# Perceiver block on one core: who spreads the softmax reciprocals over the columns, how Pool splits the second context, and where the second block of keys and values stands

## The reference

```python
q = split_heads(layernorm(x) @ Wq + bq)            # x: (2, 128, 512)
k = split_heads(ctx @ Wk + bk)                      # ctx: (2, 2048, 512)
v = split_heads(ctx @ Wv + bv)
attn = softmax(einsum('bhqd,bhkd->bhqk', q, k) / sqrt(32), axis=-1)
x = x + (einsum('bhqk,bhkd->bhqd', attn, v) as (2, 128, 512)) @ Wo + bo
x = x + self_attention(layernorm(x));  x = x + expert_ffn(layernorm(x))
```

## Time and profile before

| what | value |
|---|---|
| median of 3 runs | 535.88 us (535.83 to 538.25) |
| the profiled execution's own time | 539.55 us |
| its span, first to last instruction | 537.8 us |
| busy: PE, DVE, ACT, Pool | 514.9, 277.7, 248.9, 41.5 us |
| mean granted TensorE clock | 0.983 of full |

### The profile page before, as it was taken

One profiled execution on the slowest core, in us unless ns is written; L12 is line 12 of the kernel. 1 busy time (PEld: TensorE's weight loads), 2 busy tenths in 40 slices (PEclk: granted clock), 3 DMA queues, 4 the chain that ended last, 5 costly groups with the idle time before them and its releaser, 6 DMA issues.

```text
span 537.8 us, 9156 instructions
## 1 busy us (share of the span) xinstructions
PE 514.9 (96%) x3702; PEld 376.3 (70%) x3702; DVE 277.7 (52%) x570; ACT 248.9 (46%) x381; POOL 41.5 (8%) x56
## 2 busy tenths in 40 slices
PE   8989999999996999999999999898999999999995
PEld 5777777777774777888877778656665446877651
DVE  3676533645456552435385774530385537976232
ACT  4230128484945541237467567484164208655120
POOL 0130000000596000000000000000000010000000
PEclk9999999999997999999999999999999998999898
DMA  8800000000620022220400000781996964873000
GB/s 259 348 0 1 1 1 1 2 1 1 230 85 1 2 79 79 79 79 1 137 3 2 1 1 1 292 335 48 394 397 241 385 238 168 328 291 153 1 20 21
DMA packets 11746, 63.30 MB, mean 118 GB/s; under 512 B 1588, under 2 KB 2612, under 8 KB 4788
## 3 DMA queue, kind: packets, MB, share of 16 engines
q1 hardware_dynamic: 11704, 62.71, 30.9%
HBM read 62.18 MB, written 0.52 MB: 117 GB/s over the span
## 4 chain that ended last, share of the span: by engine, by line
PE 86%; ACT 7%; issue 2%; DVE 2%; DMA 1%; SPq 1%; POOLq 0%; DVEq 0%; ACTq 0%
PE ps L1004 36%; PE ps L1070 10%; PE ps L1259 10%; PE ps L1084 5%; PE ps L1058 5%; PE ps L1306 5%; ACT Pm L393 3%; PE ps L1286 3%; PE ps L1287 3%; PE ps L1288 3%; PE ps L998 1%; ACT PT L401 1%; DMA wv_raw<-in_xWv 1%; DVE rexp L666 1%; PE ps L1269 1%
## 5 line engine op out<-in xcount | busy, mean ns | idle before, releaser
L401 ACT COPY PT<-ps 128x512 f32<-128x512 f32 x128 | 68.8, 590 | 37.4 <-PE ps L1070 37.4
L655 DVE TENSOR_SCALAR_CACHE_REDUCE Pm<-ps,small 128x512 f32<-128x512 f32 x96 | 66.4, 748 | 29.4 <-PE ps L1058 29.2
L1070 PE MATMUL ps<-ident,Pm 128*128 128x128 f32 x512 | 69.7, 278 | 3.1 <-ACT Pm L393 2.2
L1070 PEld LDWEIGHTS ps<-ident,Pm 128*128 128x128 f32 x512 | 56.5, 141 | 18.4 <-issue 12.5
L393 ACT ACTIVATE Pm<-Pm,small 128x2048 f32<-128x2048 f32 x32 | 64.3, 2009 | 10.2 <-DVE Pm L655 10.1
L1259 PE MATMUL ps<-w1raw,z 128*128 128x512 f32 x128 | 57.3, 595 | 0.7 <-DVE Pm L655 0.7
L635 DVE SCALAR_TENSOR_TENSOR KrL<-ps,small,KrH 128x512 fp32r<-128x512 f32 x32 | 23.9, 747 | 56.8 <-ACT KrH L379 56.8
L1004 PE MATMUL ps<-ctxH,wkH 128*128 128x512 f32 x124 | 52.5, 423 | 0.0
L1004 PE MATMUL ps<-wvH,ctxH 128*128 128x512 f32 x124 | 49.8, 401 | 0.0
L1004 PE MATMUL ps<-ctxH,wkL 128*128 128x512 f32 x124 | 49.4, 399 | 0.0
L1004 PE MATMUL ps<-ctxL,wkH 128*128 128x512 f32 x124 | 49.4, 398 | 0.0
(11 more groups left out here) (169 smaller groups left out, 763.6 us busy)
## 6 DMA issues: line engine op xcount, KB each, us to landing
w1raw<-in_W SPq DMA_DIRECT2D x16, 1024.0 KB, 7.0
w2raw<-in_W SPq DMA_DIRECT2D x16, 1024.0 KB, 5.0
raw<-in_ctxT SPq DMA_DIRECT2D x7, 1024.0 KB, 4.9
woF<-in_ffn_Wo SPq DMA_DIRECT2D x4, 1024.0 KB, 12.3
wo<-in_wo SPq DMA_DIRECT2D x2, 1024.0 KB, 6.6
ctx_first<-in_ctxT SPq DMA_DIRECT2D x4, 256.0 KB, 5.0
wv_raw<-in_xWv SPq DMA_DIRECT2D x2, 512.0 KB, 6.9
wq<-in_xWq SPq DMA_DIRECT2D x1, 1024.0 KB, 12.0
```

The lines of the kernel that those rows point to most:

```text
L401: act.copy(PT[:, c % 2, i, :, :].rearrange("p k t -> p (k t)"), ps[:, T_BANKS[i % 2], :]).then_inc(pt_done, 1)
L655: dve.tensor_scalar(Pm[:, i, c * CH:(c + 1) * CH], ps[:, i, :], -1.0, mx[:, p % 2, i, c - 1:c] if c else NOT_YET, ALU.mult, ALU.min, accum ...
L1070: last = pe.transpose(ps[:, T_BANKS[i % 2], j * P:(j + 1) * P], Pm[:, i, c * CH + j * P:c * CH + (j + 1) * P], ident[:])
```

## The change

Four edits, and the wait counts that go with them:

1. `rexp`, the reciprocals spread over 32 columns a head, is written by a new ACT function `reciprocals(p)`, not by DVE. DVE's `reciprocals(p)` keeps only the four reciprocals. A new semaphore `recip_done` goes from DVE to ACT, and `rexp_done` now counts one a pass.
2. The place: DVE makes `reciprocals(p - 1)` behind `negative_scores(p, 2)` in every pass; before, it made those of pass `p - 2` at the loop's start, but for passes 4 and 8. ACT spreads them in chunk 3, between its second and third copy of transposed probabilities.
3. Pool splits each chunk of the second context with one cast and one subtraction of 128x2048, in place of four and four of 128x512.
4. The opening: PE makes `keys(0, 1)` ahead of the query projections, `values(0, 1, 0)` ahead of `scores(0, 0)`, and the other three blocks of values behind it. DVE and ACT take their part of `keys(0, 1)` ahead of their work on the queries.

```diff
@@ Pool
-                for k in range(KT):
-                    pool.tensor_copy(ctxH[c][:, k, :], raw[c][:, k, :]).then_inc(ctx_hi1, 1)
-                for k in range(KT):
-                    pool.wait_ge(ctx_hi1, KT * c + k + 1)
-                    pool.tensor_tensor(ctxL[c][:, k, :], raw[c][:, k, :], ctxH[c][:, k, :].bitcast(F32), ALU.subtract)\
-                        .then_inc(ctx_split1, 1)
+                pool.tensor_copy(ctxH[c][:], raw[c][:]).then_inc(ctx_hi1, 1)
+                pool.wait_ge(ctx_hi1, c + 1)
+                pool.tensor_tensor(ctxL[c][:], raw[c][:], ctxH[c][:].bitcast(F32), ALU.subtract).then_inc(ctx_split1, 1)
@@ ACT
+            keys(0, 1)
             act.wait_ge(bq_scaled, 1)
...
+            def reciprocals(p):
+
+                act.wait_ge(recip_done, p + 1)
+                if p:
+                    act.wait_ge(r_mm, p)
+                act.copy(rexp[:], recip.rearrange("p (h o) -> p h o", o=1).to_broadcast([P, HPG, DH])).then_inc(rexp_done, 1)
...
                         probs_T(p - 1, c, i)
+                        if c == 3 and i == 1:
+                            reciprocals(p - 1)
@@ DVE
             def reciprocals(p):
                 dve.wait_ge(exp_done, HPG * (p + 1))
-                dve.reciprocal(recip, den[:, p, :]).then_inc(rexp_done, 1)
-                dve.wait_ge(rexp_done, 2 * p + 1)
                 if p:
-                    dve.wait_ge(r_mm, p)
-                dve.tensor_copy(rexp[:], recip.rearrange("p (h o) -> p h o", o=1).to_broadcast([P, HPG, DH]))\
-                   .then_inc(rexp_done, 1)
+                    dve.wait_ge(rexp_done, p)
+                dve.reciprocal(recip, den[:, p, :]).then_inc(recip_done, 1)
...
-                if late:
-                    reciprocals(p - 2)
...
-                    if c == 2 and p in (G, NP):
+                    if c == 2:
                         reciprocals(p - 1)
@@ PE
-                pe.wait_ge(rexp_done, 2 * (p + 1))
+                pe.wait_ge(rexp_done, p + 1)
...
+            keys(0, 1)
             pe.wait_ge(xT_done, B)
             pe.wait_ge(wq_in, 16)
             for m in range(G):
                 product(ps[:, (m + 2) % 4, 0:TOK], [(wq[:, k, m * P:(m + 1) * P], xnT[:, k, :]) for k in range(KT)])\
                     .then_inc(q_mm, 1)
+            values(0, 1, 0)
             pe.wait_ge(q_split, G)
             scores(0, 0)
-            for c in range(1, C):
+            for j in range(1, JT):
+                values(0, 1, j)
+            scores(0, 1)
+            for c in range(2, C):
                 keys(0, c)
```

More of the change, by code:

```diff
@@ L214, in perceiver_block @@
         pt_done = sem("pt_done")
+        recip_done = sem("recip_done")
         pv_mm, rexp_done, r_mm, r_copied, o_done = (
@@ L426, in _ @@
             for c in range(1, C):
-                keys(0, c)
+                if c > 1:
+                    keys(0, c)
                 for j in (0, 2):
@@ L1010, in keys @@
                 if b:
-                    pe.wait_ge(ctx_split1, KT * (c + 1))
+                    pe.wait_ge(ctx_split1, c + 1)
                 else:
```

## The result

| | before | after |
|---|---|---|
| median | 537.07 us (535.83 to 539.99, 4 runs) | 529.95 us (528.53 to 530.43, 4 runs) |
| profiled execution, its span | 539.55, 537.8 us | 528.53, 526.8 us |
| mean granted clock in it | 0.983 | 0.998 |

The ratio is 0.9845, with a 95% interval of 0.9811 to 0.9879: 6.5 to 10.2 us saved. The two medians lie 7.1 us apart, inside that interval; one of the four executions of the changed kernel is the profiled one.

What follows compares the result with a forecast made beforehand. PE was taken to set the time, busy 514.9 of 537.8 us. Terms -7.3, +0.4 and -0.8 made -7.7 us, 539.55 to 531.9; less 3.67 from profile to median, 528.2, rounded to 528.4, range 526.6 to 531.4.

Steps and rivals of the forecast that it cites:

- The copy leaves DVE: Pass 4's start: without the held `rexp` copy, 5.21 us of PE gap and 2.15 of slow matmuls go; minus 7.3 us.
- ACT's copy 0.26 us, hidden but for 0.4 at pass 4's end: ACT's spread: idle time hides it before other passes' exponentials; pass 4's last weighted values wait, plus 0.4 us.
- rival B: ACT slips in every pass because its spread takes 1.2 us: 3.1 us lost, 531.5 us; chance 3%.
- The reciprocal is not held: Pass 3: DVE's reciprocals, moved into Pool's stretch, stay at 172 to 179 ns and cost nothing.
- rival D: Pass 3: Pool holds DVE's reciprocal in place of the copy, delaying the exponentials: 537.2 to 539.2 us; chance 2%.
- Edit 3 is worth zero: Pool's whole pieces end its run some 2 us sooner, but off PE's path: zero.
- The opening: PE gaps of 0.73 and 1.39 us go, one of 1.3 comes before the fourth values block: minus 0.8 us.
- rival C: Opening: DVE's copy of values comes in time and PE keeps the whole 2.1 us: 526.9 us; chance 8%.
- Minus 7.7 in all, 528.4 us: Whole kernel: -7.3 + 0.4 - 0.8 us, taken off the profile, then shifted to the median and rounded.
- Rival A: Pass 4's stall is smaller without the profiler: 531.9 us, or 530.3 with only the slow matmuls missing; chance 15%.

Runs made afterwards that it cites:

- e1: Kernel before, with only the reciprocals made a chunk sooner and spread by ACT; Pool in slices and opening as before: ratio 0.9887.
- e5: Changed kernel with Pool's split of the second context back in slices: ratio 0.9863.
- e3: Kernel before plus one wait: Pool starts the second context's chunk 3 only after DVE's copy to `rexp` of pass 2: ratio 0.9865.
- e2: Kernel before with reciprocals and the copy to `rexp` moved behind `negative_scores(p, 2)`, the copy still on DVE: ratio 1.0046.
- e4: Kernel before with only the new order of the opening: ratio 0.9984.
- e8: Changed kernel with the spread to `rexp` back on DVE, in the new place: ratio 0.9815.
- e10: Kernel before with DVE's reciprocals and copy moved behind `negative_scores(p, 2)`, each Pool cast slice followed by its own subtraction: 531.71 us, one execution.
- e11: Changed kernel with the spread back on DVE, and DVE's copy of `values(0, 1, 1)` put ahead of `split(2)`: ratio 0.9784.
- e12: Kernel before with DVE's reciprocals and copy moved behind `negative_scores(p, 2)`, Pool's casts whole, subtractions in four slices: 532.43 us, one execution.
- e9: Kernel before with DVE's reciprocals and copy moved behind `negative_scores(p, 2)`, Pool's casts and subtractions in halves of 1024 columns: 534.73 us, one execution.
- e7: Kernel before with only Pool's split in whole pieces: ratio 0.9876.

## Why the prediction was right, and where it was not

- *The copy leaves DVE: minus 7.3 us.* Right in mechanism and sum: 7.34 in the change, e1 and e5 (e3 shows the cause). The split is less right than it looks. From the gap's end to pass 4's scores the slow clock cost 10.15 - 7.67 = 2.5 us and not 2.15, since the 2.15 counts `keys(4, 1)` alone and the clock was at half to 175.22. Against that, a pass 4 that comes on time waits about 0.4 us for ACT's exponentials at the last transposes ahead of its scores, which the late pass hid. Both were left out, and that they cancel, so that 5.21 + 2.15 met 7.31, is luck.
- *ACT's copy 0.26 us, hidden but for 0.4 at pass 4's end.* It took 0.30, and PE waited 0.29 there; the other passes keep their 27.6 us, so rival B fell.
- *The reciprocal is not held* (rival D). Right: 173 to 179 ns, and 0.17 us ahead of the held copy in e2.
- *Edit 3 is worth zero.* Right beside edits 1 and 2 (e5), but the reason beside it was too broad. "The copy is held until Pool has finished its whole run of slices" was read from one copy. It holds for the order of the kernel before (also in e2 and e4); with whole pieces the wait ends with one instruction (e8), which is what the Trainium skill (SBUF — State Buffer, Who interferes with whom) says of every such wait. The traces agree with it in e8, e10, e11 and e12 (0.73 to 1.08 us) and disagree before and in e2, e4 and e9 (3.28 to 10.15 us). The prediction weighed that rule and the row against each other as if one had to be wrong. Alone edit 3 brings 5.2 us (e7), and with edits 2 and 3 in place edit 1 adds nothing (e8).
- *The opening: minus 0.8.* The gap ahead of the fourth block of values came as worked out, with DVE's copy as its releaser, 1.01 us and not 1.3, and the gain was 1.12. So rival C fell (its 526.9 takes the 1.3 off 528.2, the sum ahead of rounding). The term was mis-sized mainly because ends of matmul groups in the timeline were added up; the queries' group reads 7.17 us, but the next group starts 6.72 after its start (26.50 to 33.22).
- *Minus 7.7 in all, 528.4 us.* Measured in the trace 8.2, by the ratio 8.3. The absolute time is 1.5 us higher, 1.2 of it since the median of before itself is 537.07 over four runs and not 535.88. Rival A, a smaller stall in ordinary executions, fell in its main form: it would have saved 4.0 us, or 5.6 with only the slow matmuls missing, and the interval begins at 6.5. A part of it may be true of single executions. Of the 23 of the kernel before beside e1, five (535.21 to 535.90 us) have a mean clock of 0.995. Over 533.8 us that leaves an estimated 5.3 us at half clock in all, less than the 6.83 of the profile behind this one gap, so the slow stretch there was shorter or missing; their traces are not kept.

## What to carry to other kernels

When a short DVE copy between SBUF tiles takes microseconds, look at what Pool does in that time; e3's two lines settle it. There are several cures (move the copy to ACT, hold Pool back, cut Pool's work otherwise), they do not add up, and moving the copy sooner without one of them can lose. When a step is put ahead of a wait, find the copy that the next bank needs: here it stood behind a 3.5 us split, and putting it first won 1.3 us more.

## What was not expected of the hardware

- Pool's instructions hold a DVE copy for anything from the rest of one instruction (0.73 to 1.08 us in all where the next border let it in) to ten borders more (10.15 us), depending on how its own work is cut, and not simply by their length.
- A PE gap of 2.50 us (e7) left the clock at 1.00, one of 5.21 (before) brought it to 0.50 for 6.8 us, of which PE was busy for 5.3.
- The same code had zero, one or two slow stretches of 1.6 us in the second half of its profile; two of them are 3.2 us of the 5.2 by which single executions of the kernel before differ (535.21 to 540.45).
